# Turning the router's normalised rows by SBUF-to-SBUF transposing transfers instead of TensorE and a ScalarE copy

## The chip, the core and the metric

The kernel runs on one core of a Trainium2 chip. The metric is device microseconds of one execution. Before the change three executions took 940.93, 936.22 and 936.63 us, median 936.63 us.

## What is computed

A transformer block over 16 batches of 256 tokens of width 256: cross attention to 77 context rows with 16 heads, then a mixture of 8 experts of which each token uses its best two.

```python
x = x + xattn(layernorm(x), ctx)               # 16 heads of 16, softmax over 77 keys
h = layernorm(x)
probs = softmax(h @ router_w)                  # [T, 8]
top_w, top_i = top_k(probs, 2)
for e in range(8):
    y = silu(h @ gate_w[e]) * (h @ up_w[e])    # width 1024
    out += cw[:, e:e+1] * (y @ down_w[e])
x = x + out
```

Float32 products are made of float16 pairs: a value is split into a high and a low float16 part, and three matmuls (high by high, high by low, low by high) give the product. Lines 556 to 558 are these three matmuls, whoever calls them.

## The kernel before

There is one instruction stream per engine, written out by hand, and all order between engines is by semaphores that are waited for in the stream of the consumer. An engine executes its stream in order, so a wait holds up everything behind it.

The attention stage runs in rounds. In each round six batches are at different stages: `n` (load, layer norm, key and value projection), `a` (query projection), `b` (scores, softmax and weighted values), `c` (output projection, residual), `r` (second layer norm, router) and `z` (routing tables and the scatter of rows to the experts' regions in HBM). A round has eight units, `u` = 0 to 7; a unit treats four heads of one half (128 tokens) of batch `b`. On TensorE (PE) a unit is: the scores of unit u+2, the values weighed for unit u-2, `take_high` of unit u-1 (L632), and `turn_probs` of unit u (L625, four transposes). The other stages' work is hung behind a given unit by the dictionary `extra`: at u=1 `turn_x` and `turn_att`, at u=2 `project_q`, at u=3 `project_o`, at u=4 `turn_x2`, at u=5 `router`, at u=7 the key and value projections. VectorE (DVE) and ScalarE (ACT) have matching dictionaries. Steady rounds begin with the first layer norm's `norm` on ACT (L920) at u=0, which is followed by `turn_x` on PE at u=1.

The router's way through a round, for batch `r`, is this. ACT normalises (L920, x2n) at u=2. DVE casts the rows to their float16 high part (L1156) at u=3. GpSimd (POOL) makes the low part (L1628); after that `row_ready` is complete. High and low parts lie side by side in `rows`, 512 float16 values per token. PE's `turn_x2` (L681) makes eight 128 by 128 transposes of them into one PSUM bank, ACT's `copy_x2` (L896) copies the bank to `x2t` in SBUF, and `router` makes 12 matmuls of 8 columns with `x2t` as the stationary operand. DVE's `route_top` takes the maximum, the shifted logits (L1230) and the two best experts. ACT's `router_exp` (L907) takes the exponentials at the end of u=7, and PE's `ranks` follows at u=0 of the next round.

SyncE (SP) issues the transfers of each round, in order: `load_a` (next batch's x and context; waits for `norm` of the batch before), `spread_keys` (eight small SBUF-to-SBUF transfers, L357), `store_c` (result rows, L449), `load_c` (residual rows, L454). POOL issues the scatters (L1648) itself.

The end of the attention stage is written out in `last_rounds`. It interleaves the last two batches' routing with the first three tiles of expert 0. SP there issues the pieces of expert 1's weights (`load_second`), each after the one before has landed, and `load_rows(0)`, `(1)` and `(2)`, which fetch the sorted rows of a tile into the single buffer `raw`. Tile 3 and all later tiles need the scatter of the last batch. Then come the experts' loops, 68 tiles in all, in which PE multiplies nearly without a break.

## Time and profile before

| | us |
|---|---|
| runs | 940.93, 936.22, 936.63 |
| span of the profiled execution, first to last instruction | 908.2 |
| median less that span | 28.4 |
| PE busy in the span | 853.4 (94%) |
| DVE busy | 608.7 (67%) |
| ACT busy | 478.5 (53%) |
| POOL busy | 298.2 (33%) |

The profiled execution is known by its span alone; its own time with what lies around the span is not listed, and the median is used for it. Mean granted TensorE clock in the span is 0.989 of full speed. The attention stage lasts until about 359 us of the span and the experts' tiles fill the rest. In a timeline row the first number is the start in us from the span's start, the second the duration in us, then engine, line, operation, what is written and read, shapes and count; a bracket tells how long the engine had been idle before it and what ended that.

### The profile page before, as it was taken

The numbers are of one execution on the slowest core, as the hardware profiler recorded it, in microseconds if no ns is written. First come the engines' busy times: TensorE is split into PE (matmuls) and PEld (weight loads), VectorE is DVE, ScalarE is ACT, GpSimd is POOL, SyncE is SP. The second block draws the span as 40 slices with busy tenths as digits, with TensorE's granted clock in tenths as the row PEclk, the third lists the DMA queues.
The fourth block names the chain that finished last, engine by engine and source line by source line (L and its number), as shares of the span: only waits on it lengthen the run. The fifth ranks groups of instructions, "written<-read, shape, count | busy, mean of one in ns | idle before, by whom it ended". The sixth has DMA issues, their size and how long they took to land.

```text
span 908.2 us, 32299 instructions
## 1 busy us (share of the span) xinstructions
PE 853.4 (94%) x12208; PEld 782.6 (86%) x12208; DVE 608.7 (67%) x1932; ACT 478.5 (53%) x900; POOL 298.2 (33%) x427
## 2 busy tenths in 40 slices
PE   4898999999999987899999999999999999999995
PEld 3777777787777777899999999999999999999995
DVE  7789889889888875675574466548546657444442
ACT  6778778888888864453353244325324335323231
POOL 4799344344443445412211222122212222122112
PEclk9999999999999999999999999999999999999998
DMA  7211322223222454652262244225324422222121
GB/s 217 83 46 47 101 80 66 82 70 98 77 67 67 143 149 122 187 153 57 50 173 35 41 96 122 35 60 126 72 58 107 105 49 36 35 35 31 30 35 18
DMA packets 72884, 74.04 MB, mean 82 GB/s; under 512 B 20748, under 2 KB 62810, under 8 KB 72826
## 3 DMA queue, kind: packets, MB, share of 16 engines
q1 hardware_dynamic: 46906, 36.08, 14.3%
q0 software_dynamic: 13536, 19.85, 12.6%
q10 hardware_dynamic: 12384, 17.35, 5.9%
q8 instruction: 35, 0.57, 0.3%
q14 instruction: 23, 0.19, 0.1%
HBM read 45.18 MB, written 26.80 MB: 79 GB/s over the span
## 4 chain that ended last, share of the span: by engine, by line
PE 72%; POOL 7%; issue 5%; DMA 5%; ACT 4%; DVE 4%; SPq 1%; ACTq 0%; POOLq 0%; DVEq 0%
PE bank L556 15%; PE bank L558 15%; PE bank L557 15%; PE bank L760 6%; PE bank L761 6%; PE bank L762 6%; PE bank L625 3%; DMA expert_rows<-rows,slot_u 2%; POOL e_stage L1578 2%; PE bank L632 2%; POOL e_lo L1586 2%; PE bank L734 2%; DMA raw<-expert_rows 1%; ACT pt_hi L885 1%; ACT xn L920 1%
## 5 line engine op out<-in xcount | busy, mean ns | idle before, releaser
L556 PE MATMUL bank<-xg,e_hi 128*128 128x128 f16 x2176 | 374.4, 220 | 1.5 <-DVE xg L1414 1.3
L557 PE MATMUL bank<-xg,e_hi 128*128 128x128 f16 x2176 | 374.3, 220 | 0.0
L558 PE MATMUL bank<-xg,e_lo 128*128 128x128 f16 x2176 | 374.2, 220 | 0.0
L1671 POOL DMA_INDIRECT out<-y_sb,tok_row x67 | 107.7, 1607 | 436.9 <-DVE y_sb L1433 411.6
L556 PEld LDWEIGHTS bank<-xg,e_hi 128*128 128x128 f16 x2176 | 213.9, 98 | 3.3 <-DVE xg L1414 1.9
L557 PEld LDWEIGHTS bank<-xg,e_hi 128*128 128x128 f16 x2176 | 213.9, 98 | 0.7
L558 PEld LDWEIGHTS bank<-xg,e_lo 128*128 128x128 f16 x2176 | 213.9, 98 | 0.0
L949 ACT ACTIVATE g_act<-bank 128x512 f32<-128x512 f32 x136 | 81.2, 597 | 235.8 <-PE bank L558 228.3
L1438 DVE SCALAR_TENSOR_TENSOR h_full<-bank,g_act 128x512 f32<-128x512 f32 x136 | 94.0, 691 | 116.5 <-ACT g_act L949 108.7
L760 PE MATMUL bank<-e_hi,h_hi 128*128 128x256 f16 x544 | 148.3, 273 | 3.4 <-DVE h_lo L1444 3.0
L761 PE MATMUL bank<-e_lo,h_hi 128*128 128x256 f16 x544 | 148.3, 273 | 0.0
L762 PE MATMUL bank<-e_hi,h_lo 128*128 128x256 f16 x544 | 148.3, 273 | 0.0
L954 ACT ACTIVATE h_hi<-h_full 128x512 f16<-128x512 f32 x136 | 85.7, 630 | 104.3 <-DVE h_full L1438 104.3
L1444 DVE TENSOR_TENSOR h_lo<-h_full,h_hi 128x512 f16<-128x512 f32 x136 | 94.3, 694 | 50.6 <-ACT h_hi L954 46.7
L912 ACT ACTIVATE pt_lo<-bank 77x512 f16<-77x512 f32 x112 | 66.2, 591 | 31.7 <-PE bank L632 30.6
L625 PE MATMUL bank<-ident,probs 128*77 128x128 f32 x512 | 78.7, 276 | 0.6 <-ACT probs L879 0.6
L1648 POOL DMA_INDIRECT expert_rows<-rows,slot_u x64 | 63.6, 994 | 46.7 <-DMA expert_rows<-rows,slot_u 26.2
L885 ACT ACTIVATE pt_hi<-bank 77x512 f16<-77x512 f32 x128 | 74.2, 579 | 0.5 <-PE bank L625 0.5
L879 ACT ACTIVATE probs<-probs 128x308 f32<-128x308 f32 x128 | 58.1, 454 | 28.4 <-DVE probs L1175 26.9
L1414 DVE COPY xg<-bank 128x512 f16<-128x512 f16 x68 | 28.8, 424 | 64.8 <-PE bank L558 61.3
L625 PEld LDWEIGHTS bank<-ident,probs 128*77 128x77 f32 x512 | 65.3, 148 | 7.1 <-ACT probs L879 1.0
L1169 DVE TENSOR_REDUCE row_max<-bank 128x4 f32<-128x308 f32 x128 | 59.7, 466 | 2.1 <-issue 1.6
(186 smaller groups left out, 1746.6 us busy)
## 6 DMA issues: line engine op xcount, KB each, us to landing
raw<-expert_rows SPq DMA_DIRECT2D x68, 132.5 KB, 2.5
e_stage<-in_gate_w ACTq DMA_DIRECT2D x24, 256.0 KB, 3.2
e_stage<-in_up_w ACTq DMA_DIRECT2D x22, 256.0 KB, 3.0
e_stage<-in_down_w ACTq DMA_DIRECT2D x20, 256.0 KB, 3.2
expert_rows<-pads SPq DMA_DIRECT2D x8, 530.0 KB, 3.8
xin<-in_x SPq DMA_DIRECT2D x16, 256.0 KB, 2.8
xres<-in_x SPq DMA_DIRECT2D x16, 256.0 KB
out<-x SPq DMA_DIRECT2D x16, 256.0 KB, 2.2
```

What stands on the lines that cost most here:

```text
L556: pe.matmul(dst, a_hi(c), b_hi(c), start=c == 0, stop=False)
L557: pe.matmul(dst, a_hi(c), b_lo(c), start=False, stop=False)
L558: mm = pe.matmul(dst, a_lo(c), b_hi(c), start=False, stop=ends and c == chunks - 1)
L625: mm = pe.matmul(ps_probs[u % 2][0:KS, h * P:(h + 1) * P], probs[:, u % 2, h, :], ident[:], is_transpose=True, start=h == 0, stop=h == HG - 1)
L760: pe.matmul(ps_y[:, 0:D], h_hi[:, f, :], e_hi[:, parity, at:at + D], start=f == 0, stop=False)
L761: pe.matmul(ps_y[:, 0:D], h_hi[:, f, :], e_lo[:, parity, at:at + D], start=False, stop=False)
L762: mm = pe.matmul(ps_y[:, 0:D], h_lo[:, f, :], e_hi[:, parity, at:at + D], start=False, stop=f == FC - 1)
L885: act.activation(pt_hi[:, u % 2, :], ps_probs[u % 2][0:KS, :], ACT.Copy).then_inc(pt_hi_ready, 1)
L954: act.activation(h_hi[:, s * FS:(s + 1) * FS, :].rearrange("p f t -> p (f t)"), h_full[:, s, :], ACT.Copy).then_inc(h_hi_ready, 1)
L1438: dve.scalar_tensor_tensor(h_full[:, s, :], ps_up[s][:], H_DOWN, g_act[:, s, :], ALU.mult, ALU.mult).then_inc(h_ready, 1)
L1444: dve.tensor_tensor(h_lo[:, s * FS:(s + 1) * FS, :].rearrange("p f t -> p (f t)"), h_full[:, s, :], h_hi[:, s * FS:(s + 1) * FS, :].rearra ...
L1671: pool.indirect_dma_start(out, bass.IndirectOffsetOnAxis(tok_from[:], 0), y_from[:], None, compute_op=ALU.add).then_inc(added, 16)
```

## The change

The eight PE transposes per batch and the ACT copy are gone. In their place SP issues, per batch, two transposing transfers (one per half of 128 tokens), each turning 128 rows of 512 float16 values (128 KB) in `rows` into four blocks of 128 by 128 in `x2t`. They wait for `row_ready` and for the router of the batch before (`logits_made`). In the rounds they stand in SP's stream between `spread_keys` and `store_c`. In the written-out end they stand at four places: for batch 12 ahead of the pieces of expert 1, for batch 13 between pieces 4 and 5, for batch 14 between pieces 7 and 8, and for batch 15 between the last `store_c` and `load_rows(2)`. PE's `router` waits for the transfers (`x2_turned`) and moves from u=5 to u=6. PE's wait for `slots_ready` goes to the head of `router`. On DVE `route_top` moves from the start of u=7 to its end. `x2t` changes its layout, with the same bytes.

```diff
-        x2t = sb("x2t", [P, KC, 2, S], F16)
+        x2t = sb("x2t", [P, 2 * KC, S], F16)
...
+            def turn_x2(r):
+
+                after(sp, row_ready, r.value(2, 2))
+                after(sp, logits_made, r.value(1))
+                apart(sp, passed)
+                for t in range(NT):
+                    sp.dma_start_transpose(x2t[:, :, t * P:(t + 1) * P],
+                                           rows[:, rows_at(r), t, 0:D].bitcast(F16)).then_inc(x2_turned, 16)
+
-            def round_of(j):
+            def round_of(j, r=None):
                 load_a(j)
                 spread_keys(j - 1)
+                if r:
+                    turn_x2(r)
                 store_c(j - 3)
                 load_c(j - 2)
...
-                    round_of(At(4 + odd, k, 2))
+                    round_of(At(4 + odd, k, 2), At(odd, k, 2))
...
             spread_keys(At(B - 1))
+            turn_x2(At(B - 4))
             sp.wait_ge(e_lo_ready, PIECES)
             load_second(range(0, 3))
             landed(sp, At(HELD_FROM))
             load_rows(0)
             store_c(At(B - 3))
             load_c(At(B - 2))
-            load_second(range(3, 7))
+            load_second(range(3, 5))
+            turn_x2(At(B - 3))
+            load_second(range(5, 7))
             store_c(At(B - 2))
             load_c(At(B - 1))
-            load_second(range(7, 9))
+            load_second(range(7, 8))
+            turn_x2(At(B - 2))
+            load_second(range(8, 9))
             load_rows(1)
             load_second(range(9, PIECES))
             store_c(At(B - 1))
+            turn_x2(At(B - 1))
             load_rows(2)
...
-            def turn_x2(r, par):
-
-                after(pe, row_ready, r.value(2, 2))
+            def router(r):
+
+                after(pe, x2_turned, r.value(16 * NT, 16 * NT))
                 after(pe, slots_ready, r.value(1))
...
-            def router(r):
-
-                after(pe, x2t_ready, r.value(1, 1))
                 first_use(r, w_lo_ready, 5)
...
-                         4: [(r, lambda r: turn_x2(r, rows_at(r)))],
-                         5: [(r, router)],
+                         6: [(r, router)],
...
-            def copy_x2(r):
-
-                after(act, x2_turned, r.value(1, 1))
-                act.activation(x2t[:].rearrange("p c l s -> p (c l s)"), ps_x2t[:].rearrange("p c l s -> p (c l s)"),
-                               ACT.Copy).then_inc(x2t_ready, 1)
-
...
-                         6: [(z, lambda j: finish(weights_chain)), (z, lambda j: finish(slots_chain))]}
+                         6: [(z, lambda j: finish(weights_chain)), (z, lambda j: finish(slots_chain))],
+                         7: [(r, lambda j: start(route_top(j)))]}
                 starts = {1: [(z, lambda j: start(weights_chain))],
-                          2: [(z, lambda j: start(slots_chain))],
-                          7: [(r, lambda j: start(route_top(j)))]}
+                          2: [(z, lambda j: start(slots_chain))]}
```

## Rows read from the trace of the kernel before

**Rows 1.** Busy time of each engine by stretches: one steady round, then the experts' stage.

```profile
core 0: us, PE busy (x) PEld busy (x) DVE busy (x) ACT busy (x) POOL busy (x), PEclk, DMA share, GB/s
232.00:251.00 19.00, 17.86 (x239) 14.89 (x236) 16.67 (x70) 15.71 (x35) 8.40 (x16) 1.00 0.27 78
...
400.00:900.00 500.00, 498.20 (x7516) 480.82 (x7513) 282.09 (x675) 184.83 (x307) 97.39 (x61) 1.00 0.32 66
```

**Rows 2.** Who waited for whom, 100 to 320 us: total, times, longest.

```profile
PEld bank L556 <- DVE probs L1175: 3.7, 12, 0.9
```

**Rows 3.** Chain that ended last, 250 to 271 us: start, us, what.

```profile
260.28 0.45 PE bank L681 x8
```

**Rows 4.** Timeline of DVE in one steady round.

```profile
259.20 0.69 DVE L1204 SCALAR_TENSOR_TENSOR x<-bank,xres 128x512 f32<-128x512 f32 x1 [0.91 <-PE bank L670]
...
262.39 0.48 DVE L1175 TENSOR_TENSOR probs<-bank,row_max 128x308 f32<-128x308 f32 x1
...
263.14 0.42 DVE L1190 TENSOR_TENSOR att<-bank,inv_sum 128x256 f32<-128x256 f32 x1
...
266.03 0.17 DVE L1230 TENSOR_TENSOR expl<-bank,top 128x16 f32<-128x16 f32 x1
...
267.82 0.69 DVE L1180 TENSOR_TENSOR pt_lo<-bank,pt_hi 77x512 f16<-77x512 f32 x1 [0.20 <-ACT pt_hi L885]
```

**Rows 5.** Timeline of ACT in the same round.

```profile
260.72 0.58 ACT L885 ACTIVATE pt_hi<-bank 77x512 f16<-77x512 f32 x1
261.20 1.01 ACT L896 ACTIVATE x2t<-bank 128x1024 f16<-128x1024 f16 x1
...
267.68 0.21 ACT L907 ACTIVATE expl<-expl 128x16 f32<-128x16 f32 x1
```

**Rows 6.** Timeline of PE in the same round.

```profile
259.68 0.60 PE L625 MATMUL bank<-ident,probs 128*77 128x128 f32 x4
260.12 0.61 PE L681 MATMUL bank<-ident,rows 128*128 128x128 f16 x8
...
261.36 0.41 PE L632 MATMUL bank<-pt_hi,minus 77*77 77x512 f16 x1
...
264.24 0.60 PE L625 MATMUL bank<-ident,probs 128*77 128x128 f32 x4
...
265.92 0.41 PE L632 MATMUL bank<-pt_hi,minus 77*77 77x512 f16 x1 [0.37 <-ACT pt_hi L885]
```

**Rows 7.** Timeline of POOL, two rounds: low parts of the rows.

```profile
238.79 1.55 POOL L1628 TENSOR_TENSOR rows<-x2n,rows 128x128 f16<-128x128 f32 x4 [4.61 <-DVE rows L1156]
257.69 1.55 POOL L1628 TENSOR_TENSOR rows<-x2n,rows 128x128 f16<-128x128 f32 x4 [4.61 <-DVE rows L1156]
```

**Rows 8.** Timeline of SP's queue in the same round.

```profile
253.38 5.11 SPq L357 DMA_DIRECT2D k_diag<-k_parts  x8
260.09 0.40 SPq L449 DMA_DIRECT2D out<-x  x1
```

**Rows 9.** What SP's queue waited for, 0 to 370 us: total, times, longest.

```profile
SPq L441 <- ACT xn L920: 128.6, 15, 12.7
```

**Rows 10.** Transfers: KB each, median us from issue to landing, whole span.

```profile
raw<-expert_rows SPq DMA_DIRECT2D x68, 132.5 KB, 2.5
```

**Rows 11.** Landing of the `raw` transfers alone, 300 to 370 us.

```profile
DMA to landing us min/median/max: 2.1/3.5/5.7
```

**Rows 12.** Timeline of PE around the last batch's router and at the experts' start.

```profile
339.82 0.62 PE L681 MATMUL bank<-ident,rows 128*128 128x128 f16 x8 [0.93 <-POOL rows L1628]
...
341.59 0.17 PE L556 MATMUL bank<-r_hi,x2t 128*128 128x8 f16 x1
...
341.89 0.38 PE L734 MATMUL bank<-ident,raw 128*128 128x128 f16 x4
...
359.06 0.40 PE L734 MATMUL bank<-ident,raw 128*128 128x128 f16 x4 [2.39 <-issue]
```

**Rows 13.** Timeline of SP's queue: the fetch of tile 2's rows.

```profile
334.75 0.34 SPq L492 DMA_DIRECT2D raw<-expert_rows  x1
```

**Rows 14.** Chain that ended last, 318 to 362 us: tile 3's rows.

```profile
354.22 2.67 DMA raw<-expert_rows
```

More of the change, by code:

```diff
@@ L219, in build @@
         ps_rank_pair = ps_r[:, NT * E:2 * NT * E].rearrange("p (t e) -> p t e", t=NT)
-        ps_x2t = ps_r[:].bitcast(F16).rearrange("p (c l s) -> p c l s", c=KC, l=2)
         ps_gate = [banks[0], banks[1]]
@@ L281, in build @@
         x2_turned = sem("x2_turned")
-        x2t_ready = sem("x2t_ready")
         logits_made = sem("logits_made")
@@ L671, in project_o @@
                 mm.then_inc(o_made, 1)
-            def turn_x2(r, par):
-                after(pe, row_ready, r.value(2, 2))
+            def router(r):
+                after(pe, x2_turned, r.value(16 * NT, 16 * NT))
                 after(pe, slots_ready, r.value(1))
-                parts = rows[:, par, :, 0:D].bitcast(F16)
-                for c in range(KC):
-                    for l in range(2):
-                        for t in range(NT):
-                            mm = pe.transpose(ps_x2t[:, c, l, t * P:(t + 1) * P],
-                                              parts[:, t, l * D + c * P:l * D + (c + 1) * P], ident16[:])
-                mm.then_inc(x2_turned, 1)
-            def router(r):
-                after(pe, x2t_ready, r.value(1, 1))
                 first_use(r, w_lo_ready, 5)
@@ L690, in router @@
                     mm = three(ps_logits[:, t, :],
-                               lambda c: x2t[:, c, 0, t * P:(t + 1) * P], lambda c: x2t[:, c, 1, t * P:(t + 1) * P],
+                               lambda c: x2t[:, c, t * P:(t + 1) * P], lambda c: x2t[:, KC + c, t * P:(t + 1) * P],
                                lambda c: r_hi[:, c, :], lambda c: r_lo[:, c, :], KC)
@@ L786, in last_rounds @@
                 turn_att(c)
-                turn_x2(r, rows_at(r))
                 gate_up(0, 0, 1, front)
@@ L798, in last_rounds @@
                 gate_up(1, 0, 1, front)
-                turn_x2(c, rows_at(c))
                 down(1, 0, 1, 1)
@@ L932, in body @@
                              (first, lambda _: norm(n, 0, xin, xn, xt_turned, 1, xn_ready, n))],
-                         4: [(r, copy_x2)],
                          7: [(r, router_exp)]}
@@ L972, in last_rounds @@
                 high_h(0, 0)
-                copy_x2(r)
                 fetch(1, ACT.Exp)
@@ L979, in last_rounds @@
                 silu_step(1, 0)
-                copy_x2(c)
                 fetch(2, ACT.Exp)
```

## The prediction

> **What bounds the kernel now.** I read the busy time by stretches first, to split the span, then the waits, then one steady round engine by engine, then the last batch. The experts' stage is TensorE alone: 498.20 of 500 us [rows 1]. The change touches nothing there, so that stage only moves as a block with its start, PE's transposes of tile 3's rows at 359.06 us [rows 12]. What can change lies before that: 14 routed batches in rounds, and batches 14 and 15 in the written-out end.
>
> In a steady round (18.9 us, from the same POOL instruction at 238.79 and 257.69 [rows 7]) PE is busy 17.86, DVE 16.67 and ACT 15.71 of 19 us [rows 1]. No engine is full, so the round's length is a loop through all three, and the question is whether `turn_x2` and `copy_x2` are links of it. In the round at 251 us PE works from `turn_x` to the end of `project_o`; that end releases the residual on DVE at 259.20, for which DVE had been idle 0.91 us [rows 4]. From there DVE shows no idle time until 267.62 (0.20 before 267.82): residual, a shift, statistics, the low query part, then the shift at 262.39 and the normalisation at 263.14, ending at 263.56 [rows 4]. PE's next scores wait for that shift: PE's weight loads waited for it 12 times in 220 us, 3.7 us in all [rows 2]. After that the loop runs between ACT and PE in the light units (PE waits 0.37 us for ACT at 265.92 [rows 6]) to the next round's norm. Between 259.20 and 263.56 DVE sets the pace, and `turn_x2` (260.12, [rows 6]) and `copy_x2` (261.20, [rows 5]) lie beside it.
>
> **The change part by part, in a steady round.**
>
> PE's eight transposes: about 0.45 us of PE's time [rows 3]. Without them the next scores could start by at most that much earlier. But `take_high` at 261.36 needs ACT's high part of the probabilities, 260.72 + 0.58 = 261.30 [rows 5, 6], which starts ahead of the ACT copy and does not move. So PE stands at the same place at 261.36. Gain 0. The cover is DVE and that ACT instruction; were it gone the gain would be up to 0.45 us.
>
> ACT's copy: 1.01 us [rows 5]. The next low part could start once `take_high` is done, some 0.3 us earlier, and the exponential after it still needs DVE's shift, ending 262.87 [rows 4]. Gain 0. The router's own wait for the copy goes too, but PE stands at its next scores until the same shift is done: gain 0.
>
> The router at u=6 instead of u=5: 12 matmuls, 0.30 us (341.59 to 341.89 for the same twelve, [rows 12]). They now follow `turn_probs` of u=6, which begins at 264.24 and holds PE 0.44 us, as at 259.68 and 260.12, so to about 264.68 [rows 6]. Behind them stand scores, weighed values and `take_high` at 265.92, before which PE is idle 0.37 us [rows 6]. 0.30 fits into 0.37. Cost 0, but only some 0.1 us of cover is left.
>
> `route_top` on DVE half a unit later: the same instructions, interleaved with the same statistics. Its shifted logits, now 266.03, would come at about 266.7; ACT takes them at 267.68 [rows 4, 5]. DVE has 0.20 us of idle time before 267.82. Cost 0, at most 0.2 us a round if the interleaving packs worse.
>
> SP's stream: the two issues wait for `row_ready`, 257.69 + 1.55 = 259.24 [rows 7]. SP has ended the keys at 258.49 and issues the store at 260.09 [rows 8]. Behind the new wait stand store, residual load and the next `load_a`; `load_a` waits for ACT's norm anyway, 128.6 us in 15 times, about 8.6 each [rows 9]. Two issues more of under 1 us each vanish in that. Cost 0; it would begin to cost when the issues together exceed some 8 us. A wait for `logits_made` of the batch before is met a round earlier.
>
> The transfers are the one thing the trace does not show. PE wants `x2t` at 264.68, that is 5.4 us after `row_ready`; over the steady rounds the two times differ by 5.3 to 5.4 us, and with the 0.1 of cover 5.5 is the threshold. From below: an ordinary 132.5 KB transfer of 128 rows lands 2.5 us after its issue [rows 10], issues take 0.40 us [rows 8], and SP reacts in 0.2 (residual done at 259.89, store at 260.09 [rows 4, 8]): 0.2 + 0.6 + 2.5 = 3.3 us, or 2.9 with the shortest landing, 2.1 [rows 11]. From above: the key spreads take 5.11 us for eight issues, 0.64 each [rows 8], with 64 short runs in each. If issue time went with the number of runs, a transfer of 512 blocks of 256 bytes would take 8 x 0.6 = 4.8 us, and two would land 0.2 + 9.6 + 2.5 = 12.3 us after `row_ready`. I take the lower side, since each transfer reads 128 rows of contiguous 1 KB like `raw`, but with the spreads' issue and the slower landing: 0.2 + 0.64 + 3.5 = 4.3 us [rows 8, 11]. That is 1.2 us inside the threshold. Sum over 14 rounds: 0, with both ends kept for the range: 0 and (12.3 - 5.5) x 14 = +95 us.
>
> The rows show that eight 128 by 128 transposes hold PE 0.45 us together [rows 3]. The Trainium skill, "VectorE: DVE Perf Modes", section "The three transpose paths", gives 390 ns for one on TensorE and 1309 ns for one by DMA, which speaks against this change. Eight by DMA, one after the other, would be an estimate of 10.5 us, 5 us a round over the threshold, and the kernel would take about 1010 us by it. For TensorE the trace disagrees with the page once the blocks follow each other (0.06 us each), so the page's DMA figure may be a latency in the same way; no run so far shows it.
>
> **The last batch.** Here there is no cover. Before: rows ready at about 339.8, for which PE waited 0.93 us, router at 341.59, tile 2's rows turned at 341.89, fetched long before (334.75) [rows 12, 13]. After: batch 14's transposes are gone from PE too, so the last residual and everything to `row_ready` come up to 0.45 us earlier, 339.3. Plus 4.3 gives 343.6 for the router instead of 341.59. SP must also finish these issues before `load_rows(2)`: 339.3 + 0.2 + 1.3 = 340.8, landing 2.5 to 3.5 later, 343.3 to 344.3. PE turns tile 2's rows at about 344.0 instead of 341.89: +2.1 us. What follows is a chain of PE, DVE and ACT to 359.06, so it comes through. Tile 3's rows, in which the last scatter's delay would show, land at 354.22 + 2.67 = 356.89 and have 2.2 us in hand [rows 12, 14]. With the fast end (2.9) the cost is about 1 us, with 7.6 about 5 us. Batches 12 to 14 have their transfers issued behind weight pieces, and those pieces a few us later; I find no first user that is near.
>
> **Sum.** 14 x 0 + 2.1 = 2.1 us. The span goes from 908.2 to 910.3; with the 28.4 us by which the median of the runs exceeds the profiled span, taken as unchanged, the time goes from 936.6 to 938.7 us.
>
> **Rivals.**
> 1. Slower: the transfers land later than 5.5 us after `row_ready`. PE then stands before the router at u=6, the loop runs through it, and every us over the threshold costs 14 us. For it: transposed writes are finer than ordinary ones, and scatters share the DMA engines in just these microseconds. Midway between 2.9 and 12.3, 7.6 us, costs 2.1 x 14 + 5 = 34 us: 971 us; the far end gives 1040. By the page named above the time would lie between these two. Chance 0.33.
> 2. Faster: PE is a link after all. The chain view puts the transposes on the chain in every steady round [rows 3]. 0.45 x 12 = 5.4 us less, with the 2.1 of the end 933.3; if the ACT copy counts too, another few us. Against it: DVE's unbroken work and PE's waits for it [rows 2, 4]. Chance 0.12.
> 3. The transfers hold back other queues' transfers, scatters above all. POOL has idle time in each round [rows 7], so this costs little; it is in the forecast's width.
>
> **How the numbers follow.** Forecast 0.55: hidden in the rounds, +1 to +4 at the end, 937 to 942. Slow transfers 0.33, of which some 0.2 lies below 966. Faster 0.12. The range 934 to 966 leaves out about 0.13 above and 0.06 below. The measurement can tell 0.5%, 4.7 us, from no change. Under 931.9: 0.08 (rival 2 with ACT's part or a cheap end). Over 941.3: rival 1 and an edge of the forecast, 0.36. Within: 0.56.
>
> **What would show it.** Right: rounds of 18.9 us; router matmuls at u=6 with no idle time before them or one that ends on DVE; landing under 5.5 us after L1628; an idle PE of about 3 us before the last router and the start at about 361 instead of 359.06. Wrong: PE idle before each router and ended by the transfer; SP issues of several us; or rounds shorter by 0.3 to 0.5 us with DVE's idle time before the residual unchanged.

## The result and the profile after

The changed kernel takes 927.86 us (median of 6 runs, 925.79 to 932.31) against 935.68 us (median of 6) for the kernel before on the same chip: ratio 0.9922, 95% interval 0.9895 to 0.9949. It is faster by 0.8%, where the prediction was 938.7 us, no change that the measurement could tell; the time lies below the predicted range of 934 to 966 us.

The page of the changed kernel, its first lines, PE, the granted clock and the DMA packets:

```profile
span 925.2 us, 32092 instructions
...
PE 856.1 (93%) x12080; PEld 781.5 (84%) x12080; DVE 611.9 (66%) x1932; ACT 465.4 (50%) x884; POOL 298.7 (32%) x427
...
PEclk9999999999999978999999999999999999999998
...
DMA packets 90292, 78.24 MB, mean 85 GB/s; under 512 B 38156, under 2 KB 80218, under 8 KB 90234
```

This execution took 927.0 us, 1.8 us more than its span. The profiled execution of the kernel before on which the prediction rests had a span of 908.2 us and stood beside runs of 936; I had put the 28.4 us between them down as a constant outside the span. It is not. The kernel before, profiled again, has a span of 933.7 us in an execution of 935.5 us. So the trace that I argued from was of an execution that lost nothing in places where the others lose some 25 us. Where these lie is the first thing to read. Times in each trace, from the starts of ACT's instructions and of PE's transposes of tile 3's rows:

| | before, first trace | before, again | changed |
|---|---|---|---|
| mean of eight steady rounds, us | 18.91 | 20.62 | 19.23 |
| batch 1's round | 21.1 | 20.7 | 23.6 |
| last exponential of the rounds at | 319.1 | 335.9 | 325.2 |
| from there to the experts' start | 40.0 | 49.8 | 50.2 |
| experts' start to the last instruction | 549.1 | 548.0 | 549.8 |
| span | 908.2 | 933.7 | 925.2 |

From the second column to the third the rounds give 10.7 us back, the written-out end costs 0.4 and the experts' stage 1.8: together the 8.5 us of the spans. The gain is in the rounds, where I had put 0.

The changed kernel by stretches, as [rows 1]:

```profile
core 0: us, PE busy (x) PEld busy (x) DVE busy (x) ACT busy (x) POOL busy (x), PEclk, DMA share, GB/s
232.00:251.00 19.00, 17.53 (x230) 14.55 (x229) 16.96 (x71) 14.96 (x33) 8.39 (x16) 0.99 0.35 96
400.00:900.00 500.00, 499.21 (x7553) 482.68 (x7554) 287.33 (x679) 188.74 (x315) 98.30 (x61) 1.00 0.32 71
```

ACT is 0.75 us less busy than in [rows 1], PE 0.33; the DMA share went from 0.27 to 0.35 (the packets of the whole kernel from 72884 to 90292). The experts' stage is PE as before.

Its steady round, engine by engine. DVE's residual and the shift and normalisation after it, as [rows 4]:

```profile
265.24 0.69 DVE L1196 SCALAR_TENSOR_TENSOR x<-bank,xres 128x512 f32<-128x512 f32 x1 [0.91 <-PE bank L685]
...
268.44 0.48 DVE L1167 TENSOR_TENSOR probs<-bank,row_max 128x308 f32<-128x308 f32 x1
...
269.19 0.42 DVE L1182 TENSOR_TENSOR att<-bank,inv_sum 128x256 f32<-128x256 f32 x1
```

The residual to the shift takes 3.20 us, in [rows 4] 3.19; DVE waits the same 0.91 us before it. PE in that stretch, as [rows 6]:

```profile
267.40 0.41 PE L647 MATMUL bank<-pt_hi,minus 77*77 77x512 f16 x1 [0.16 <-ACT pt_hi L886]
...
268.97 0.30 PE L571 MATMUL bank<-k_diag,q_hi 128*128 128x308 f16 x1 [0.73 <-DVE probs L1167]
...
270.28 0.60 PE L640 MATMUL bank<-ident,probs 128*77 128x128 f32 x4
270.72 0.17 PE L571 MATMUL bank<-r_hi,x2t 128*128 128x8 f16 x1
```

Where the transposes stood PE now waits: 0.16 us for ACT's high part and 0.73 us for DVE's shift, and the router comes at u=6 with no wait. SP's queue and POOL in the round of 243 us, as [rows 7, 8]:

```profile
243.89 1.55 POOL L1620 TENSOR_TENSOR rows<-x2n,rows 128x128 f16<-128x128 f32 x4 [4.60 <-DVE rows L1148]
...
245.55 2.52 SPq L469 DMA_TRANSPOSE x2t<-rows  x2
...
247.29 1.04 POOL L1640 DMA_INDIRECT expert_rows<-rows,slot_u  x1 [0.53 <-issue]
...
248.64 0.97 POOL L1640 DMA_INDIRECT expert_rows<-rows,slot_u  x1 [0.31 <-issue]
...
251.13 0.21 PE L571 MATMUL bank<-r_hi,x2t 128*128 128x8 f16 x1
...
251.19 0.97 POOL L1640 DMA_INDIRECT expert_rows<-rows,slot_u  x1 [1.58 <-DMA expert_rows<-rows,slot_u]
...
253.22 0.97 POOL L1640 DMA_INDIRECT expert_rows<-rows,slot_u  x1 [1.05 <-issue]
```

SP reacts 0.11 us after the low parts end (245.44) and is busy 2.52 us with the two issues; the router starts 5.69 us after the low parts. The fourth scatter starts 2.03 us after the third.

The kernel before, profiled again, in its round of 221 us: ACT, PE and POOL where it loses.

```profile
235.45 0.45 ACT L879 ACTIVATE probs<-probs 128x308 f32<-128x308 f32 x1
235.52 0.98 POOL L1648 DMA_INDIRECT expert_rows<-rows,slot_u  x1 [1.49 <-DMA expert_rows<-rows,slot_u]
...
236.43 0.41 PE L632 MATMUL bank<-pt_hi,minus 77*77 77x512 f16 x1 [0.37 <-ACT pt_hi L885]
...
236.80 0.97 POOL L1648 DMA_INDIRECT expert_rows<-rows,slot_u  x1 [0.30 <-issue]
...
238.40 0.59 ACT L912 ACTIVATE pt_lo<-bank 77x512 f16<-77x512 f32 x1 [2.02 <-remote]
238.90 0.45 ACT L879 ACTIVATE probs<-probs 128x308 f32<-128x308 f32 x1
```

PE starts `take_high` at 236.43 and is done some 0.4 us later, but ACT, which waits for just that, starts its low part only at 238.40, after 2.02 us of idle time; an undisturbed round shows 0.50 us there. The releaser is called "remote", that is none that the profile finds in time. From one exponential to the next (the seventh unit of the round, u=6, called unit 7 from here) that makes 3.45 us where the first trace has 1.93. In the trace's semaphore events three of PE's increments, due at 236.06, 236.84 and 237.28 (the ends of their matmuls), arrive together at 238.35 to 238.44; no other engine's is seen late there. Two scatters, 1.28 us apart, start at 0.07 and 1.35 us into this unit. The first trace has the two scatters at the same places and no late semaphore: in its eight steady rounds all 312 of PE's increments come within 0.1 us of the ends of their matmuls, while in this one 61 are over 0.25 us late or missing from the record, and most of the late ones arrive 1.5 to 1.8 us after a scatter's start. That was the new hypothesis (H): PE's semaphores are held up while POOL puts out scatters, and the change helps because its scatters 3 and 4 lie further apart, 1.7 to 2.7 us in the steady rounds of its trace. The rivals: F, the work taken off PE and ACT; M, the router's later place.

### The profile page after: what moved, and what is told of

The parts are those of the page before. It is cut to its first block, busy times and chain, and to the rows that moved or that the text cites. A ratio compares the mean times of both kernels' runs of the same rounds, so it can differ in the third digit from the quotient of the medians.

```text
span 925.2 us, 32092 instructions
## 1 busy us (share of the span) xinstructions
PE 856.1 (93%) x12080; PEld 781.5 (84%) x12080; DVE 611.9 (66%) x1932; ACT 465.4 (50%) x884; POOL 298.7 (32%) x427
## 2 busy tenths in 40 slices
DMA packets 90292, 78.24 MB, mean 85 GB/s; under 512 B 38156, under 2 KB 80218, under 8 KB 90234
## 4 chain that ended last, share of the span: by engine, by line
PE 59%; issue 2%; DVE 2%; DMA 2%; ACT 1%; POOL 1%; SPq 0%; another core or an unknown queue 0%; DVEq 0%; POOLq 0%; ACTq 0%
PE bank L571 13%; PE bank L573 13%; PE bank L572 13%; PE bank L763 6%; PE bank L764 6%; PE bank L765 6%; PE bank L737 2%; DMA raw<-expert_rows 1%; PE bank L647 0%; DMA expert_rows<-rows,slot_u 0%; DVE e_lo L1295 0%; DVE h_lo L1436 0%; PE bank L640 0%; DVE h_full L1430 0%; ACT pt_hi L886 0%
## 5 line engine op out<-in xcount | busy, mean ns | idle before, releaser
L640 PE MATMUL bank<-ident,probs 128*77 128x128 f32 x512 | 81.1, 282 | 0.6 <-ACT probs L880 0.6
L640 PEld LDWEIGHTS bank<-ident,probs 128*77 128x77 f32 x512 | 67.4, 153 | 7.6 <-issue 1.2
L763 PEld LDWEIGHTS bank<-e_hi,h_hi 128*128 128x128 f16 x544 | 53.4, 98 | 9.7 <-DVE h_lo L1436 4.8
```

What stands on the lines that cost most here:

```text
L640: mm = pe.matmul(ps_probs[u % 2][0:KS, h * P:(h + 1) * P], probs[:, u % 2, h, :], ident[:], is_transpose=True, start=h == 0, stop=h == HG - 1)
L763: pe.matmul(ps_y[:, 0:D], h_hi[:, f, :], e_hi[:, parity, at:at + D], start=f == 0, stop=False)
```

## The experiments

All were timed in five rounds beside the kernel before on the same chip; a ratio is to that kernel, with its 95% interval. "Round" is the mean of eight steady rounds in the profiled execution. The groups ran on four chips, so kernels of different groups are compared by their ratios (before_single and before_single_loop, for one).

| kernel | us | ratio | round |
|---|---|---|---|
| before_again | 936.3 | 1.0016 [0.9994, 1.0038] | 20.62 |
| move_only | 936.2 | 1.0005 [0.9975, 1.0035] | 20.54 |
| after_again | 928.4 | 0.9915 [0.9883, 0.9948] | 19.64 |
| after_pe8 | 931.7 | 0.9952 [0.9928, 0.9977] | 19.63 |
| after_pe8_act | 934.7 | 0.9984 [0.9955, 1.0013] | 20.10 |
| after_pair | 934.4 | 0.9978 [0.9950, 1.0006] | 20.31 |
| after_last_pe | 926.9 | 0.9909 [0.9876, 0.9943] | 19.39 |
| before_single | 925.0 | 0.9888 [0.9862, 0.9914] | 18.98 |
| before_single_loop | 921.0 | 0.9844 [0.9809, 0.9879] | 19.01 |
| single_loop_mid | 922.2 | 0.9867 [0.9835, 0.9898] | 18.95 |
| single_loop_mid_again | 920.9 | 0.9847 [0.9816, 0.9878] | 18.95 |
| single_loop_end | 922.9 | 0.9859 [0.9822, 0.9895] | 19.16 |
| after_single | 931.1 | 0.9943 [0.9914, 0.9973] | 19.67 |
| after_single_work | 933.1 | 0.9977 [0.9950, 1.0005] | 19.37 |
| after_mid | 930.4 | 0.9929 [0.9902, 0.9956] | 19.60 |
| after_best | 929.0 | 0.9933 [0.9908, 0.9958] | 19.60 |
| after_late | 959.7 | 1.0254 [1.0220, 1.0288] | 22.20 |
| after_late_single | 946.5 | 1.0116 [1.0081, 1.0150] | 21.33 |

**Is the freed work the gain?** Both kernels once more, and the changed kernel with the work put back for batches 0 to 13.

before_again and after_again are the two kernels unedited. The expectations of these first four were written before hypothesis H was formed; it came out of before_again's trace.

> The kernel before, unchanged, for a trace from the same chip and session as the changed kernel's. Its profiled span before was 908.2 us against a median of 935.7, the changed kernel's 925.2 against 927.9, so the two traces are not of like executions. Theory A (the old trace was of an execution with a higher granted TensorE clock or fewer stalls than the timed ones): the span comes out near 934 us, with a lower mean clock than 0.989, and the lost time sits in stretches of lower clock. Theory B (the time around the span differs between the kernels): the span is again near 908 and the time near 936.

> The changed kernel, unchanged, beside the next two. Expected: ratio to before 0.992, some 928 us; the last router again waits about 4.5 us for its transfers and the second routed batch about 4.8 us.

Of the first, theory A had the span right and the place wrong: the rounds between 160 and 242 us take 20.2 to 20.5 us each at a granted clock of 1.00, so the loss in unit 7 is not one of the clock. Of the second, the ratio came out; the last router waits 4.8 us for its transfers, batch 1's does not wait at all, and batch 0's waits 1.9 us. Two of its rounds have scatters 3 and 4 close together, as in the kernel before. POOL, PE and ACT in the first of them:

```profile
192.34 0.97 POOL L1640 DMA_INDIRECT expert_rows<-rows,slot_u  x1 [1.52 <-DMA expert_rows<-rows,slot_u]
...
193.22 0.41 PE L647 MATMUL bank<-pt_hi,minus 77*77 77x512 f16 x1
...
193.62 0.97 POOL L1640 DMA_INDIRECT expert_rows<-rows,slot_u  x1 [0.30 <-issue]
...
195.35 0.59 ACT L907 ACTIVATE pt_lo<-bank 77x512 f16<-77x512 f32 x1 [2.18 <-remote]
```

They lie 1.28 us apart (1.48 in the other round), and unit 7 takes 3.60 us (3.45) where its neighbours with 1.7 us and more between the two take 1.92 to 2.73. So the changed kernel loses in the same way where its scatters fall as before, which is H within one kernel.

after_pe8 adds PE's eight transposes at u=4, their result unused:

```diff
...
+                         4: [(r, lambda r: turn_again(r, rows_at(r)))],
                          6: [(r, router)],
...
```

> The changed kernel with the eight PE transposes per batch put back at u=4 for batches 0 to 13 (their result is not used; the transfers still feed the router). Theory P (PE's freed 0.45 us per round is the gain): 14 x 0.45 = 6 us slower than the changed kernel, 934 us. Theory D (DVE sets the pace there, as I argued): same as the changed kernel within 1 us. Theory C (the gain is a higher granted clock because PE has gaps or works less): slower by some us, with more lower-clock stretches in the trace.

after_pe8_act adds ACT's copy of 128x1024 too, which the router waits for:

```diff
...
+                         4: [(r, copy_again)],
                          7: [(r, router_exp)]}
...
```

> As the one before, and ScalarE's copy of the bank (128x1024) is put back too at u=4; the router at u=6 waits for it as well. All the old work is back for batches 0 to 13 while the transfers and the later router stay. Theory P and A together (the freed PE and ScalarE time is the gain): 6 to 12 us slower than the changed kernel, back at 936 or above. Theory M (the gain comes from the router's and route_top's later place, not from the freed work): same as the changed kernel, 928 us. Theory D: same as the changed kernel within 1 us.

Put back, the work takes the gain away in two steps, of about 3.5 and 3 us. The intervals of after_again and after_pe8 overlap, those of after_again and after_pe8_act do not. Taken alone that speaks for F. But the undisturbed units have the same lengths in all four traces and add up to 18.88 us a round. What differs is how many units are disturbed: nine rounds lie 14.4 us above 9 x 18.88 in before_again and 2.8 us in the changed kernel's first trace. In after_pe8 the unit ahead of unit 7 takes 2.70 instead of 2.02 us in five of its eight steady rounds. ACT and POOL in one of them:

```profile
193.21 0.97 POOL L1656 DMA_INDIRECT expert_rows<-rows,slot_u  x1 [0.30 <-issue]
...
194.69 0.59 ACT L902 ACTIVATE pt_hi<-bank 77x512 f16<-77x512 f32 x1 [0.66 <-remote]
```

ACT goes on 1.48 us after the second scatter's start (1.47 to 1.55 us in all such rounds of both kernels), released by "remote": again a semaphore of PE that comes late after a scatter. The changed kernel's two traces have no such wait at this place. So the work does not lengthen a round as such, and the runs after these went for the disturbance. Why the put-back work brings one more semaphore into it was not found.

**Is it the move?** The kernel before with the router at u=6 and `route_top` begun at the end of u=7:

```diff
-                         5: [(r, router)],
+                         6: [(r, router)],
...
```

> The kernel before with the move alone: the router at u=6 instead of u=5, route_top begun at the end of u=7; TensorE's transposes and ScalarE's copy stay. Theory H (the rounds lose time where a scatter of GpSimd holds back TensorE's semaphores, and the changed kernel's scatters 3 and 4 lie further apart): the scatters stay 1.28 us apart, so no gain, 0.998 to 1.005 of before (934 to 940 us). Theory M (the place of the router is what brings the gain, since it takes 0.30 us of TensorE's work out of the half of the round that is short of time): 0.992 to 0.995. Theory F (freed work): no gain, as under H, so this run tells M from the two others.

No effect: 1.0005, rounds of 20.54 us, unit 7 as long as in before_again (3.3 to 3.6 us in seven of eight rounds). M is out as the source of the gain. What the later router costs when the scatters go out singly was not tested by itself.

**Is it the scatters?** The kernel before, with each scatter of a round started when the one just before it has landed:

```diff
-                    scatter(z, z.plus % 2, 2)
+                    scatter(z, z.plus % 2, 1)
```

> The kernel before, whose scatters in the rounds now each wait for the one just before them to have landed (one in flight instead of two), and nothing else. Theory H: the starts of scatters 3 and 4 go from 1.28 us apart to 2 us or more, semaphores of TensorE are held for under 1 us each, and the rounds lose some 8 us less of the 14.7 us that they lie above 18.88 us each in the profiled execution of before run again: 0.989 to 0.995 of before (926 to 931 us). Theory F (the gain is TensorE's 0.45 us and ScalarE's 1.01 us a batch): those are still there, so 0.998 to 1.003. If a held semaphore comes from any scatter, wherever it lies, more scatters now fall on the waits of u=6 and u=7 and it is slower, over 1.003.

0.9888: at least the whole gain of the change (0.9915 on the same chip, with overlapping intervals), with all of PE's and ACT's work in place. The rounds come down to 18.98 us. And the reverse, the changed kernel whose third scatter waits for the second too, so that 3 and 4 again start 1.28 us apart:

```diff
...
+                        if pair and m == 2:
+                            after(pool, scattered[1], r.value(SCATTER, 16))
...
```

> The changed kernel, whose third scatter of a batch in the rounds now waits for the second to have landed too, so that scatters 3 and 4 start 1.28 us apart as they do before; nothing else. Theory H: the rounds lose as much as those of before do, some 8 us: 0.998 to 1.003 of before (933 to 939 us), against 0.992 of the changed kernel as it is. Theory F: 0.990 to 0.994, as the changed kernel, since the freed work stays freed.

0.9978: the gain is gone, as H has it, though the work stays off. Both runs came out as H said and against F (0.9978 lies just under H's 0.998, 0.9888 just under its 0.989). Two reservations. In after_pair the pair starts some 2 us later than in before, so most of the time is lost in the first unit of the next round (up to 3.8 us instead of 2.30) and only some in unit 7. And its granted clock is lower: 0.95 over its eight steady rounds, where the changed kernel has 0.98; its rounds without a stretch of low clock still take 19.8 to 19.9 us, where the changed kernel's take 18.9 to 19.2.

**The last batch.** The changed kernel with batch 15 turned by PE and copied by ACT as before; the core of the edit:

```diff
...
-            turn_x2(At(B - 1))
...
+                turn_last(c, rows_at(c))
...
-                router(c)
+                router(c, True)
...
```

> The changed kernel with its last batch (15) alone turned as before: 8 transposes of TensorE (0.45 us) and a copy of ScalarE (1.0 us) in place of the two transposing transfers, which TensorE waited 4.5 us for in both profiled executions of it. If that wait is on the path to the experts' stage, the time falls by 2 to 4 us against the changed kernel (924 to 926 us, 0.988 to 0.990 of before); if what follows (the router's chain on VectorE, the tables) has slack, it falls by under 1 us.

926.9 against 927.9 and 928.4: 1.0 to 1.5 us, with intervals that overlap. From the last exponential to the experts' start it needs 49.6 us, the changed kernel 50.2 and 49.5. The expectation was 2 to 4 us or under 1; the wait is there, but most of it is made up behind it.

**Do the two gains add?** The changed kernel with single scatters, and the same with the work put back:

```diff
-                    scatter(z, z.plus % 2, 2)
+                    scatter(z, z.plus % 2, 1)
```

> The changed kernel with each scatter of the rounds started only when the one before it has landed (the edit that took before to 0.9888). Theory H (the changed kernel's gain is only the wider spacing of its scatters): the two gains do not add; it comes to what the single scatters gave to before, 0.987 to 0.991 (923 to 927 us). Theory F (the freed work of TensorE and ScalarE is worth 7 us of its own): the gains add, 0.980 to 0.983 (917 to 920 us).

> As after_single, and batches 0 to 13 also make the 8 transposes (result not used) and ScalarE's copy of 128x1024 at u=4 again, which the router waits for. Theory H: with the scatters out of the way the undisturbed round is 18.88 us with or without this work, so it is within 0.002 of after_single. Theory F: slower than after_single by 0.45 us to 1.5 us in each of 14 batches, that is by 6 to 20 us, 0.007 to 0.02 more.

They do not add, and neither theory had the number: H expected 0.987 to 0.991. after_single is at 0.9943, slower than before_single (0.9888), which has the same scatters and the old transposes: the intervals meet at 0.9914 and no further. The work put back costs 2.0 us more by the medians (0.0034, where H allowed 0.002 and F asked for 0.007 and more), with overlapping intervals, and the profiled rounds of after_single_work are the shorter ones (19.37 against 19.67). Both ends are 5 us longer than the others' (55.0 us from the last exponential to the experts' start), while before_single, whose single scatters reach into batches 12 and 13 as theirs do, needs 49.1; so it takes both the transfers and those scatters. The next edit leaves these batches out.

**The better version.** before_single_loop has single scatters in the loop's ten rounds only:

```diff
-                    scatter(z, z.plus % 2, 2)
+                    scatter(z, z.plus % 2, 1 if z.reg is not None else 2)
```

> As before_single, but batch 0, whose scatters landed 3.4 to 6.2 us apart and held GpSimd and the keys of the next batch up (one round of 24.0 us against 21.1), keeps two in flight. Expected: that round falls by 2 to 3 us, so 0.985 to 0.989 (922 to 925 us); if the round is long for another reason, 0.989 as before_single.

921.0 us, 0.9844: the fastest kernel of the study, 0.8% faster than the changed one, with no transposing transfer in it. Of the reason that I gave little shows: the profiled before_single has 18.6 and 24.0 us for batch 1's round and the next, this one 22.5 and 18.9, 1.2 us less for the two. after_best has the same scatters and batch 15 by PE, in the changed kernel:

> The changed kernel with single scatters in the rounds but for batch 0, and its last batch turned by TensorE and ScalarE as before. Expected, if all three add to the changed kernel's own: 0.984 to 0.988 (921 to 924 us). If theory F holds too, under 0.982.

0.9933, where 0.984 to 0.988 was expected, and above before_single_loop on the same chip with intervals that do not overlap. Nothing adds to the changed kernel; its rounds stay at 19.60 us.

**Does the place in the round decide?** A memset of 128x800 by POOL, once between the first landing and the second scatter, once behind the fourth:

```diff
...
+                    if r.reg is not None and m == 1:
+                        pool.memset(idle[:], 0.0)
...
```

> As before_single_loop, with a memset of 128x800 by GpSimd (0.7 to 0.8 us) between the landing of the first scatter and the start of the second, in the ten rounds of the loop. In before_single the second scatter starts 13.8 to 14.1 us into a round, with 18.9 to 19.1 us for the round; in after_single it starts 14.8 us into it (the first takes 4.47 us to land, not 3.88), with 19.6 to 19.8. Theory P (what counts is where a scatter starts in the round, relative to TensorE's short matmuls, whatever engine or transfer put it there): the start goes to 14.6 to 14.9, those rounds to 19.5 to 19.8, 5 to 8 us more than before_single_loop, 0.990 to 0.993 of before. Rival (the transposing transfers load something that a late scatter doesn't): no change from 0.984.

> The control to single_loop_mid: the same memset, behind the fourth scatter, so that GpSimd has the same work and no scatter starts later. Theory P: 0.983 to 0.986 of before, as before_single_loop. If GpSimd's own time in a round is what counts, it comes out like single_loop_mid, 0.990 to 0.993.

0.9867 and 0.9859: the same. Theory P, in the form "a second scatter at 14.6 to 14.9 us into the round costs 0.7 us", fell. The memset put it 14.9 to 15.7 us into the round, past the sensitive place, and the rounds are 18.95 us. (The numbers that this expectation starts from hold for some rounds only: the second scatter starts 13.8 to 14.3 us into the round in before_single, 13.8 to 14.8 in after_single.) The traces say what the sensitive place is. single_loop_mid_again, the repeat that is reported below, where nothing is lost (PE, POOL, ACT):

```profile
248.36 0.41 PE L633 MATMUL bank<-pt_hi,minus 77*77 77x512 f16 x1 [0.37 <-ACT pt_hi L886]
...
248.71 0.98 POOL L1651 DMA_INDIRECT expert_rows<-rows,slot_u  x1 [0.17 <-issue]
...
248.80 0.59 ACT L913 ACTIVATE pt_lo<-bank 77x512 f16<-77x512 f32 x1 [0.50 <-PE bank L633]
```

The scatter starts when `take_high` is nearly through, and ACT goes on after 0.50 us. after_mid, the changed kernel with the same two edits:

```profile
213.97 0.76 POOL L1642 MEMSET idle<- 128x800 f16 x1 [2.89 <-DMA expert_rows<-rows,slot_u]
214.05 0.18 PE L572 MATMUL bank<-r_hi,x2t 128*128 128x8 f16 x1 [0.31 <-DMA x2t<-rows]
...
214.90 0.98 POOL L1643 DMA_INDIRECT expert_rows<-rows,slot_u  x1 [0.16 <-issue]
...
215.06 0.39 PE L648 MATMUL bank<-pt_hi,minus 77*77 77x512 f16 x1
...
216.28 0.59 ACT L908 ACTIVATE pt_lo<-bank 77x512 f16<-77x512 f32 x1 [1.53 <-PE bank L648]
```

Here the scatter starts 0.16 us ahead of `take_high`, and ACT waits 1.53 us, until 1.38 us after the scatter's start; with two scatters 1.28 us apart (above) it was 1.60 us after the second one's. The granted clock is 1.00 in this stretch. So in these traces the loss falls on a matmul whose semaphore is waited for and that ends within about 1.4 us after a scatter's start. The place alone does not settle it. With single scatters and `take_high` 1.0 us into unit 7, the unit takes 1.92 or 1.93 us when a scatter starts 0.8 us or more into it, and 1.96 to 2.21 us at 0.1 to 0.25 us. But at 0.3 to 0.7 us six such units of the kernels without the transfers (before_single_loop, single_loop_end) are undisturbed, and nine of those with them (after_mid, after_best, after_single_work) take 2.26 to 2.55 us. In the round of after_mid shown here `take_high` comes 1.23 us into the unit: the router's twelve matmuls (0.31 us) stand ahead of it, and they waited 0.31 us for the transfers.

> The changed kernel with the two edits of single_loop_mid: one scatter in flight in the rounds of the loop, and the memset of 0.8 us between the first landing and the second scatter. Over all profiled executions so far the seventh unit of a round takes 1.92 to 1.93 us when no scatter starts within its first 0.7 us, 2.0 to 2.7 with one there, 3.2 to 3.6 with two in it 1.3 us apart. The memset moves the second scatter to 0.8 to 1.7 us into it, so the rounds should be 18.9 to 19.1 us as in single_loop_mid. Theory H (the freed work of TensorE and ScalarE is worth nothing): as single_loop_mid, or worse by the last batch's and batch 1's waits for the transfers: 0.986 to 0.991 of before. Theory F: below 0.983.

> single_loop_mid once more, as the version without the transposing transfers that after_mid is compared with on the same chip: 0.983 to 0.990 of before (919 to 925 us), faster than the changed kernel's 0.992.

0.9929 against 0.9847 on the same chip; the expected rounds of 18.9 to 19.1 us did not come. In four of the eight steady rounds of after_mid `take_high` is late, 1.23 to 1.63 us into unit 7; in the other four the second scatter starts only 0.3 to 0.6 us into it, where single_loop_mid_again has 0.8 to 1.7. (That expectation's list of unit lengths also leaves out the first trace of the kernel before, with two scatters in the unit and 1.93 us.) With single scatters in both, the change costs some 9 us: 5.0 up to the last exponential (1.9 before the steady rounds, 5.2 in the eight of them at 19.60 against 18.95, 2.1 gained back behind them), 2.0 in the end and 2.4 after it, by the two spans of 928.4 and 919.0. How much of it is the transfers and how much the router's place at u=6, which all kernels with the transfers share, was not tested apart.

**What do the transfers leave to spare?** SyncE's store and load issued ahead of the transfers instead of behind:

```diff
-                if r:
-                    turn_x2(r)
                 store_c(j - 3)
                 load_c(j - 2)
+                if r:
+                    turn_x2(r)
```

> The changed kernel; in the rounds of the loop SyncE issues the store of x2 and the load of the residual ahead of the two transposing transfers, as they stand ahead of nothing in before (262.5 and 263.3 us in the round that the changed kernel issues them at 268.6 and 269.3, in the midst of the scatters). Two scatters stay in flight. Theory Q (these two transfers of 256 KB, held up behind row_ready, are what slows the landing of the first two scatters unequally and so spreads scatters 3 and 4): the spacing falls back towards 1.28 us and the time towards before, 0.996 to 1.002. Rival (the transposing transfers themselves spread them): 0.991 to 0.993, as the changed kernel.

> As after_late with one scatter in flight in the rounds of the loop. Theory Q: the first scatter lands in 3.9 us again, the second starts 14.1 us or less into the round, the rounds are 18.9 to 19.1 us, so 0.985 to 0.989 of before. Rival (the transposing transfers themselves delay the scatter): the second starts at 14.5 or later, 0.991 to 0.995, as after_single.

Neither of the theories had this in view: 1.0254 and 1.0116. after_late, POOL, SP's queue and PE in a round:

```profile
223.67 1.55 POOL L1620 TENSOR_TENSOR rows<-x2n,rows 128x128 f16<-128x128 f32 x4 [5.08 <-DVE rows L1148]
...
226.45 0.40 SPq L452 DMA_DIRECT2D xres<-in_x  x1
227.07 2.56 SPq L469 DMA_TRANSPOSE x2t<-rows  x2
...
232.74 0.18 PE L571 MATMUL bank<-r_hi,x2t 128*128 128x8 f16 x1 [1.96 <-DMA x2t<-rows]
```

The low parts end at 225.22, but the store waits for the residual of another batch, so the transfers go out at 227.07, 1.85 us late. They land for PE 5.67 us after their issue (4.6 to 5.8 in the twelve rounds of the loop), and PE stands 1.96 us before the router (0.9 to 2.7). So the threshold is real: a router that waits lengthens the round. The granted clock falls too, to 0.89 over the eight steady rounds from 0.98 in the changed kernel, so not all of the 31 us is the wait itself. The test of Q is spoilt: the scatters did go back to 1.28 us apart in after_late, but everything else had shifted as well. Why scatters 3 and 4 lie further apart in the changed kernel stays open.

The changed kernel itself does not run at the threshold. In its steady rounds the DMA packets of the two transfers are through 3.3 us after the first issue (in after_late 3.5 to 4.7), and its router asks for them 5.3 to 5.9 us after it. The semaphore comes after the last packet: where PE waited, the router started 0.6 to 1.4 us behind that packet in the changed kernel's first trace and in after_late, at most 2.1 us in after_again. That makes an estimate of 3.9 to 4.7 us from the issue, 5.4 with the longest delay; PE shows no wait before the router in any steady round of either trace.

## Why the prediction was wrong

**The step that failed** is the sum's 14 x 0 for the rounds, and with it the step from the span to the time: "the 28.4 us by which the median of the runs exceeds the profiled span, taken as unchanged". The runs showed in its place that the 28.4 us are not outside the span: all executions profiled later lie 1.7 to 1.9 us above their spans. Some 25 us lay inside it, in the rounds (17 us up to the last exponential) and in the end (10 us), less 1 in the experts' stage, and the change altered the first: the rounds gave 10.7 us back where 0 stood. A gap of 3% between the profile and the runs was among the facts at the start, and I made nothing of it. With it in doubt, neither the gain of 0 in the rounds nor the range's lower edge, 934, could be stood for: the 18.9-us round was that of the one trace, not of the runs.

**Rival 3**, the transfers' effect on the scatters, was named and priced as "this costs little". By after_pair and before_single that is the term which decided the sign. I looked only at whether POOL has idle time, at what a late scatter costs POOL; its price lay with PE's semaphores, and it was a gain against the kernel before, whose scatters lie worse.

**Gain 0 for the freed PE and ACT work in an undisturbed round**: right. The units that make 18.88 us are there with and without it, DVE's 3.2 us from residual to shift unchanged, PE waiting 0.73 us for the shift where it had transposed. Rival 2 had the direction, by luck and not by its mechanism: after_pair loses the gain with the work off, before_single has it with the work on. What stays open is how the put-back work costs after_pe8 and after_pe8_act 3.5 and 6.5 us. Their traces show it in part as late semaphores after the second scatter, not as longer undisturbed units; a part of the measured gain may hang on the freed work in this way.

**The router's place at no cost**: right with the scatters as they stood, 1.0005. `route_top` the same.

**SP's issues**: taken as under 1 us each, measured 1.26 us (1.19 to 1.63), 2.5 us for the pair; no cost in the steady rounds, as predicted. In batch 1 they queue behind eight key spreads and PE waited 3.4 us in the first trace, where that round took 23.6 us; in after_again it did not wait, and the round took 20.1. I had costed only the rounds with SP idle.

**The landing**: estimated 4.3 us after `row_ready`, with 2.9 and 12.3 as ends and 5.5 as the threshold. In the steady rounds the transfers go out 0.1 us after `row_ready` and their packets are through 3.3 us later; with the delay to the semaphore (above) that is some 4.0 to 4.8 us, an estimate, and PE never waited there. So nothing measured speaks against size or threshold, but the size is partly luck: the two issues take 2.5 us, where the sum holds one of 0.64, and the data came sooner behind them than I had put. Elsewhere it is longer: 5.0 us in the last batch, 4.6 to 5.8 from the issue in the loop of after_late, which is 31 us slower than the changed kernel. The first rival's condition, a landing later than 5.5 us, was met there and not in the changed kernel's steady rounds.

The Trainium skill's 1309 ns for a transpose by DMA ("VectorE: DVE Perf Modes", "The three transpose paths"), times eight, an estimate of 10.5 us, is not borne out as a landing time: in the last batch the eight blocks landed 4.9 us after the first issue.

**The chances** do not fit each other: 0.08 is given for under 931.9 us and 0.06 for under 934, which holds the former.

**The last batch**: +2.1 us predicted. The changed kernel, POOL, SP's queue and PE, as [rows 12, 13]:

```profile
346.25 2.00 POOL L1620 TENSOR_TENSOR rows<-x2n,rows 128x128 f16<-128x128 f32 x4 [5.04 <-DVE rows L1148]
348.35 2.50 SPq L469 DMA_TRANSPOSE x2t<-rows  x2
350.89 0.58 SPq L501 DMA_DIRECT2D raw<-expert_rows  x1
353.29 0.19 PE L571 MATMUL bank<-r_hi,x2t 128*128 128x8 f16 x1 [4.53 <-DMA x2t<-rows]
...
354.12 0.61 PE L737 MATMUL bank<-ident,raw 128*128 128x128 f16 x4 [0.34 <-DMA raw<-expert_rows]
...
375.42 0.40 PE L737 MATMUL bank<-ident,raw 128*128 128x128 f16 x4 [1.97 <-issue]
```

From the end of the low parts, 348.25, to the router it is 5.0 us, in before_again 1.8 (358.59 to 360.41); tile 2's rows follow 5.9 instead of 2.1 us after it. So the delay at this place is 3.2 to 3.8 us, rather more than I said. But "a chain of PE, DVE and ACT to 359.06, so it comes through" is wrong: from tile 2's rows to tile 3's it is 17.2 us in the first trace, 21.3 here and 25.0 in before_again, whose PE stands in gaps of 0.3 to 1.2 us in that stretch, put down to issue. Those gaps begin while POOL issues scatters 1.3 us apart (five from 365.9 to 371.0 us); the first trace has such a row of scatters too (346.9 to 352.4 us) and no gap there, as with the semaphores. The clock adds to it: from the last exponential to the experts' start it is 0.96 in the first trace, 0.86 in before_again and 0.83 here. 0.4 us of the delay is left at the experts' start, in keeping with after_last_pe.

## What to carry to other kernels

Before a sum is made on a trace, set its span against the times of the runs: a difference of some per cent is time that the trace does not show, and a change may act on just that. Work that lies beside a loop of waits is worth nothing by its size; the order in which a GpSimd scatter and a short matmul with a waited-for semaphore fall in time was worth more here than a microsecond of freed work on two engines. A transposing transfer wants its issue time, its landing and what stands ahead of it in its queue counted together: 5.4 us to its consumer were enough here with nothing ahead of it, and not when it went out 1.9 us late.

## What the hardware showed

- Semaphores of PE arrive up to 2.3 us late while POOL issues an indirect scatter: 1.38 us after the start of a single one (after_mid), 1.60 us after the second of a pair 1.28 us apart (before_again). What holds them was not found. The first trace of the kernel before, with its scatters in the same places, has no late one among 312, so it depends on something that neither the program nor these runs vary on purpose.
- A transposing transfer of 128x512 two-byte elements within SBUF holds SP's queue 1.26 us. The packets of a pair are through 3.3 us after the first issue in the steady rounds of the changed kernel; where PE waited for it, a pair landed 4.9 us after it in the last batch and 4.6 to 5.8 us in the loop of after_late. The packets are small: 17408 more for 32 transfers, 544 each.
- The granted clock of the changed kernel is 0.50, the lower level of 1.2 GHz, from 250.5 to 253.9 us, with PE at work in the steady rounds before it; PE's group of four transposes at 250.40 took 0.94 us instead of 0.60. Its two longest steady rounds (19.8 and 19.9 us) hold such a stretch. Its mean, 0.977, is lower than before_again's 0.982, in spite of which it is faster.
